# Five attention blocks of a fused transformer stack: the wait of an element's first scores is split, and its second part stands at the middle unit

## The chip, the cores and the metric

The kernel is one program for one core of a Trainium2 chip. Its time is the device time of one execution in microseconds (us). Before the change three runs gave a median of 1972.47 us (1972.38 to 1973.41). A trace was taken of one further execution, which took 1972.66 us; its span from the first to the last instruction is 1970.9 us.

## The reference

Four small transformer layers run one after the other on `x` of shape (8, 112, 256): 8 batch elements of 112 tokens. Three of them also read a context of shape (8, 375, 256). Cut to what matters:

```python
def attention(q_in, kv_in):                 # per layer with its own norm, bias, head size
    q, k, v = heads(q_in @ wq), heads(kv_in @ wk), heads(kv_in @ wv)
    s = einsum('bhqd,bhkd->bhqk', q, k) / sqrt(dh)
    return merge(softmax(s, -1) @ v) @ wo

x = x + self_attention(ln(x))               # layer 0, 16 heads of 16
x = x + cross_attention(ln(x), ln(ctx))
x = x + mixture_of_8_experts_top2(ln(x))
x = x + causal_self_attention(ln(x))        # layer 1, 16 heads of 16
x = x + mlp(ln(x))
x = x + cross_attention(ln(x), ctx)
x = x + mlp(ln(x))
x = x + cross_attention(rms(x), ctx)        # layer 2, 16 heads of 64 on 4 key heads, q and k normed
x = x + swiglu(rms(x))
x = x + self_attention(rms(x))
x = x + swiglu(rms(x))
x = x + cross_attention(rms(x), rms(ctx))   # layer 3, 16 heads of 64, rotary, plus the input mask
x = x + silu_gated_mlp(rms(x))
```

All of it is in float32.

## The kernel before

The 13 lines of the reference are 13 blocks that the kernel works through in order. In the code they are `L0_sa`, `L0_ca`, `L0_moe`, `L1_sa`, `L1_m1`, `L1_ca`, `L1_m2`, `L2_ca`, `L2_m1`, `L2_sa`, `L2_m2`, `L3_ca`, `L3_m` (`sa` self attention, `ca` cross attention). Every engine has its own program and its own in-order queue; they meet through semaphores only. Nothing schedules the work: the order on each engine is that of the Python loops.

An attention block handles the 8 batch elements in turn. Work on an element is cut into units. In `L0_ca`, `L1_ca` and `L3_ca` a unit is one head, 16 units to an element; in `L2_ca` there are 12 units and in `L2_sa` 4. Step `s` of element `b` does the following, each on its own engine: TensorE (PE) computes the scores of units `s` and `s+1` at every even `s` (`scores`, lines 882 to 926; the matmuls are on L907, L912 and L902); VectorE (DVE) takes a unit's maximum (L1762, or L1751 with the mask) and, later, the reciprocal of its row sum (L1767); ScalarE (ACT) does the exponential (L1340); GpSimd (POOL) multiplies the probabilities by the reciprocal (L2102); TensorE turns them (L935), VectorE copies them back (L1776), and TensorE multiplies them by the values (L963, L968). Each of these runs some units behind the scores. In the two steps that follow the third or so, the output projection of the element before is done (L990), and VectorE adds it to X.

Between these, the pieces of the next element `b+1` are made in the steps that the table `SCHEDULES` names: `XT` and `CT0`, `CT1` turn tokens and context, `Q`, `K0`, `K1`, `QP0`, ..., `V1` are projections, and `QT0`, `QT1`, `KT0`, `KT1` are turned queries and keys. TensorE writes a piece to PSUM (`piece`), and ScalarE copies it to SBUF (evacuates it) and then increments one of the semaphores `w_done0`, `w_done1`, `w_done2`, one for each bank that the pieces share in turn. `KT0` and `KT1` are evacuated by L1320, after the exponential of the same step.

The queries and keys of an element lie in SBUF in two halves. The first half of the units reads only the first half: in the blocks with heads of 16, `qz[..., 0:4]` and `kT[..., 0]`, in the others the queries of `QT0` and the keys of `KT0` (or `K0`). The second half of the units reads only the second. In `L0_ca` and `L1_ca` the queries are spread out with a mask by two operations on GpSimd, `spread0` and `spread1` (L623), one for each half; each increments `spread`. In `L1_ca` they stand ahead of the scaling of units 11 and 13 in GpSimd's queue, in `L0_ca` ahead of 12 and 14.

At unit 0 of an element the function `scores` waits for all of this: for both spreads (`count(st["spread"], 2, b, 2)`, L889 to L890), for the evacuation of all pieces of queries and keys (`wait_evacuated`, which for each bank waits for the last piece of those named), and, in every unit, for the banks of PSUM to be free (`exped` or `maxed`). In `L1_ca` the keys come from memory (`kv_loaded`).

Of the kernel before, what the change touches and what calls it, by code (L numbers as in the profile page):

```python
# [185 lines left out]
def parity(m):  # L186
    return (m if isinstance(m, int) else m.o) % 2

def pair(m):  # L190
    return m // 2 if isinstance(m, int) else m.i + m.o // 2
# [110 lines left out]
def build(nc, x, ctx, mask, consts, rows, b2, rbias, rows_hbm, results_hbm, keys_hbm, values_hbm, attn_w, mlp_w, out):  # L302
    with ExitStack() as es:
# [3 lines left out]
        def sem(name):  # L307
            return es.enter_context(nc.semaphore(name))
# [137 lines left out]
        spread = sem("spread")  # L446
# [109 lines left out]
        def head_of(u):  # L556

            return 8 * (u // 8) + 2 * (u % 4) + u // 4 % 2

        def place(blk, u):  # L560

            if not blk.pairs or blk.keys_first:
                return u
            if blk.dh == 64:
                return 8 * (u // 8) + 4 * (u % 2) + u % 8 // 2
            return 4 * (u // 4) + (0, 2, 1, 3)[u % 4]

        def group_of(blk, s):

            if blk.pairs:  # L570
                return 2 * (s // (2 * blk.kc)) + s % 2, s % (2 * blk.kc) // 2
            return divmod(s, blk.kc)
# [10 lines left out]
        def count(base, per, b, k=0):  # L583

            if isinstance(b, int):
                return b * per + (base + k)

            return b.i * (2 * per) + max(b.o * per + base + k, 1)
# [18 lines left out]
        def evacuated(blk, st, m, name):  # L607

            w = blk.bank_of[name]
            return w_done[w], count(st[f"w{w}"], blk.in_bank(w), m, blk.in_bank(w, name) + 1)  # L610

        def wait_evacuated(eng, blk, st, m, names):

            for w in range(len(blk.w_banks)):
                mine = [x for x in names if blk.bank_of[x] == w]
                if mine:
                    eng.wait_ge(*evacuated(blk, st, m, max(mine, key=blk.pieces.index)))
# [11 lines left out]
        def wait(eng, s, value):  # L629
            if isinstance(value, int) and value <= 0:  # L630
                return
            eng.wait_ge(s, value)
# [158 lines left out]
        def _(pe):  # L791
# [4 lines left out]
            def attention(n):  # L796
                blk, st = BLOCKS[n], START[n]
                warm = WARM.get(blk.name, {})
                spare = 7 if blk.out_bank != 7 else blk.w_banks[1]
                np_, units, gu, lag = len(blk.pieces), blk.units, blk.gu, blk.lag  # L800
# [82 lines left out]
                def scores(b, s):  # L883

                    n = 2 if blk.pairs else 1
                    free = masked if blk.mask == "causal" else maxed if blk.mask else exped
                    base = st["masked"] if blk.mask == "causal" else st["turn"] if blk.mask else st["unit"]
                    wait(pe, free, count(base, units, b, s + n - blk.s_banks))
                    if s == 0 and blk.dh == 16 and blk.cross:  # L889
                        pe.wait_ge(spread, count(st["spread"], 2, b, 2))  # L890
                    if s == 0 and blk.ahead:
                        pe.wait_ge(kv_loaded[parity(b)], pair(b) * 32 + 32)
                    if s == 0:

                        wait_evacuated(pe, blk, st, b, [x for x in blk.pieces if x in ("Q", "Q0", "Q1", "K0", "K1", "QT0", "QT1", "KT0", "KT1")])
                    if blk.pairs:
                        for z in range(2):
                            bank = blk.bank_at(s + z)
                            if blk.keys_first:
                                g, q = group_of(blk, s + z)  # L900
                                rows = slice(64 * z, 64 * z + 64)
                                mm(ps[0:blk.kp, bank, 0:HG * S], kT[rows, parity(b), g // 2, q * blk.kp:(q + 1) * blk.kp],  # L902
                                   qz[rows, parity(b), 4 * (g // 2):4 * (g // 2) + 4], start=True, stop=True).then_inc(scored, 1)
                            elif blk.dh == 16:
                                h = head_of(place(blk, s + z))
                                rows = slice(64 * z, 64 * z + 64)
                                mm(ps[0:S, bank, 0:blk.nk], qz[rows, parity(b), 4 * (h // 8) + h % 4],  # L907
                                   kT[rows, parity(b), h // 8, 0:blk.nk], start=True, stop=True).then_inc(scored, 1)
                            else:
                                u = place(blk, s + z)  # L910
                                rows = slice(64 * z, 64 * z + 64)
                                mm(ps[0:S, bank, 0:blk.nk], qz[rows, parity(b), 4 * (u // 8) + u % 4],  # L912
                                   kT[rows, parity(b), u // 8, 0:blk.nk], start=True, stop=True).then_inc(scored, 1)
                        return
                    if blk.keys_first:
                        g, q = divmod(s, blk.kc)
                        mm(ps[0:blk.kp, blk.bank_at(s), 0:HG * S], kT[:, parity(b), g // 2, q * blk.kp:(q + 1) * blk.kp],
                           qz[:, parity(b), HG * g:HG * (g + 1)], start=True, stop=True).then_inc(scored, 1)
                        return
                    for i in range(blk.heads):  # L920
                        u = s * blk.heads + i
                        last = mm(ps[0:S, blk.bank_at(s), i * blk.nk:(i + 1) * blk.nk],
                                  qz[:, parity(b), head_of(u) if blk.dh == 16 else u],
                                  kT[:, parity(b), u // 8, 0:blk.nk], start=True, stop=True)
                    last.then_inc(scored, 1)
# [82 lines left out]
                def body(b):  # L1008
                    for s in steps(b, blk, blk.out_step + 1):
                        if b == B and s in warm.get("tail", {}):  # L1010
                            keep_busy(spare, warm["tail"][s])
                        if b != B and (s % 2 == 0 or not blk.pairs):
                            scores(b, s)
                        at = lagged(b, s, lag, units)
                        if at and not blk.keys_first:
                            turn(*at)
                        if b == B and feeds(n) and s == lag - 1 + blk.keys_first:
                            pe.wait_ge(exped, START[n + 1]["unit"])
                            keep_busy(spare, warm.get("tokens", 0))
                            for b2_ in range(SOON):  # L1020
                                turn_tokens(n + 1, b2_)
                        at = lagged(b, s, lag + 1 - blk.keys_first, units)
                        if blk.keys_first and s == blk.out_step and b != 0:
                            project(b + -1, min(b + 1, B) if isinstance(b, int) else b + 1)
                        if at and at[1] % (gu * blk.wg) == gu * blk.wg - 1:
                            weigh(at[0], at[1] // gu)
                        if not blk.keys_first and s == blk.out_step and b != 0:
                            project(b + -1, min(b + 1, B) if isinstance(b, int) else b + 1)
                        if more(b):
                            for name in blk.plan.get(s, []):  # L1030
                                piece(b + 1, name, count(st["out"], 1, b) if name not in blk.early else None)
# [1278 lines left out]
```

## Time and profile before

| | us |
|---|---|
| median of three runs | 1972.47 |
| the profiled execution | 1972.66 |
| its span | 1970.9 |
| TensorE busy in the span | 1742.6 (88%) |
| VectorE busy | 1298.0 (66%) |
| ScalarE busy | 843.0 (43%) |
| GpSimd busy | 705.1 (36%) |

The five attention blocks that the change touches stand at these places (us from the start of the span; engine columns are busy time, the last is the clock granted to TensorE, 1.00 being its full 2.4 GHz):

| block | stretch | length | TensorE | VectorE | GpSimd | clock |
|---|---|---|---|---|---|---|
| `L0_ca` | 139 to 353 | 214 | 194.97 | 154.89 | 115.86 | 0.98 |
| `L1_ca` | 782 to 950 | 168 | 147.36 | 143.07 | 113.51 | 1.00 |
| `L2_ca` | 1030 to 1260 | 230 | 215.57 | 136.20 | 80.19 | 1.00 |
| `L2_sa` | 1353 to 1505 | 152 | 128.30 | 107.69 | 5.12 | 0.92 |
| `L3_ca` | 1600 to 1890 | 290 | 261.13 | 190.49 | 148.71 | 0.98 |

A wait costs time where the engine that waits sets the pace and nothing behind it has room to spare. So the rows to read are those of an element's first scores: what TensorE did before them, how long it stood idle, and what released it.

### The profile page before, as it was taken

To read this page: it belongs to the slowest core of one execution; us is meant where nothing else is said; L and a number is where in the kernel's file an instruction comes from. 1 tells how busy PE (TensorE), PEld (TensorE's weight loads), DVE (VectorE), ACT (ScalarE), POOL (GpSimd) and SP (SyncE) were. 2 spreads that over 40 slices of the span, in tenths; PEclk is the share of its full clock that TensorE was granted. 3 is DMA by queue.
4 is the path that set the end of the run, shared out by engine and by line. 5 is a ranking of instruction groups with operands and counts; after the bars stand their busy time and mean duration, and the time that the engine had idled before them with its cause. 6 is when DMAs were issued, how large, how long until landed. Compare 5 with 4: busy or idle time off the path is not lost.

```text
span 1970.9 us, 35184 instructions
## 1 busy us (share of the span) xinstructions
PE 1742.6 (88%) x11106; PEld 1235.4 (63%) x11106; DVE 1298.0 (66%) x3310; ACT 843.0 (43%) x2473; POOL 705.1 (36%) x796
## 2 busy tenths in 40 slices
PE   5979998889997888988799999898888989999998
PEld 4756665679975667555674444585445955555567
DVE  5866677511137876888775565896778966666675
ACT  3645554333335643666324443342232445445431
POOL 2325555220022234676423332340001435555443
PEclk9989999789998989999999999999999989999999
DMA  4100000388961001102100020101001000000200
GB/s 173 37 23 13 16 8 16 108 293 323 322 230 69 0 1 32 33 31 74 70 9 17 16 72 0 54 1 65 0 0 61 16 1 13 23 11 11 75 1 19
DMA packets 37006, 115.13 MB, mean 58 GB/s; under 512 B 3345, under 2 KB 23729, under 8 KB 29729
## 3 DMA queue, kind: packets, MB, share of 16 engines
q1 hardware_dynamic: 34352, 107.33, 15.7%
q0 software_dynamic: 2544, 6.43, 1.0%
q8 instruction: 59, 0.97, 0.2%
q14 instruction: 51, 0.41, 0.1%
HBM read 99.34 MB, written 14.40 MB: 58 GB/s over the span
## 4 chain that ended last, share of the span: by engine, by line
PE 41%; DVE 20%; issue 18%; POOL 14%; ACT 4%; DMA 2%; DVEq 0%; POOLq 0%; SPq 0%; ACTq 0%
POOL arena L2102 10%; PE ps L1057 6%; PE ps L1097 5%; PE ps L1207 4%; PE ps L1219 4%; PE ps L862 3%; PE ps L990 2%; PE ps L857 2%; PE ps L968 2%; DVE arena L1784 2%; PE ps L842 2%; ACT arena L1340 2%; PE ps L902 1%; PE ps L935 1%; PE ps L835 1%
## 5 line engine op out<-in xcount | busy, mean ns | idle before, releaser
L2102 POOL TENSOR_TENSOR arena<-arena,rinv 112x375 f32<-112x375 f32 (+1 forms) x448 | 370.6, 829 | 470.4 <-DVE rinv L1767 459.7
L935 PEld LDWEIGHTS ps<-cst,arena 112*125 112x125 f32 (+1 forms) x1408 | 183.8, 180 | 167.7 <-POOL arena L2102 81.9
L935 PE MATMUL ps<-cst,arena 112*125 112x112 f32 (+1 forms) x1408 | 242.6, 289 | 39.6 <-POOL arena L2102 36.5
L1340 ACT ACTIVATE arena<-ps,negmax 112x375 f32<-112x375 f32 (+1 forms) x384 | 190.3, 501 | 159.2 <-DVE negmax L1762 158.8
L1776 DVE COPY arena<-ps 125x336 f32<-125x336 f32 x384 | 190.4, 496 | 39.3 <-PE ps L935 37.8
L1762 DVE TENSOR_REDUCE negmax<-ps 112x1 f32<-112x375 f32 (+1 forms) x288 | 158.1, 549 | 69.2 <-PE ps L907 61.9
L1340 ACT ACTIVATE arena<-arena,negmax 112x112 f32<-112x112 f32 (+1 forms) x256 | 125.5, 491 | 138.9 <-DVE negmax L1751 93.0
L1057 PE MATMUL ps<-h_split_sb,w_split_sb 128*128 128x448 f32 x768 | 171.9, 371 | 7.7 <-DVE h_split_sb L1620 3.0
L1057 PEld LDWEIGHTS ps<-h_split_sb,w_split_sb 128*128 128x128 f32 x768 | 145.0, 190 | 23.8 <-POOL w_split_sb L2178 4.9
L857 PE MATMUL ps<-wat,arena 128*125 128x256 f32 (+1 forms) x576 | 145.3, 388 | 8.9 <-ACT arena L1279 7.5
L990 PE MATMUL ps<-wat,arena 128*112 128x256 f32 x512 | 126.5, 392 | 9.4 <-DVE arena L1786 3.7
L2178 POOL TENSOR_TENSOR w_split_sb<-wml,w_split_sb 128x512 fp32r<-128x512 f32 (+1 forms) x40 | 46.4, 1161 | 243.8 <-ACT w_split_sb L1406 241.9
L907 PE MATMUL ps<-arena 64*112 64x375 f32 x512 | 114.6, 525 | 16.9 <-ACT arena L1340 9.3
L1784 DVE RECIPROCAL arena<-ps 128x448 f32<-128x448 f32 x32 | 94.5, 2952 | 50.7 <-PE ps L976 50.7
L857 PEld LDWEIGHTS ps<-wat,arena 128*125 128x125 f32 (+1 forms) x576 | 101.5, 187 | 38.4 <-issue 17.0
L1097 PE MATMUL ps<-g_split_sb,w_split_sb 128*128 128x448 f32 x480 | 111.2, 368 | 5.0 <-DVE g_split_sb L1909 5.0
L990 PEld LDWEIGHTS ps<-wat,arena 128*112 128x112 f32 x512 | 87.1, 179 | 39.0 <-issue 8.4
L1767 DVE RECIPROCAL rinv<-rowsum 112x1 f32<-112x1 f32 (+1 forms) x448 | 70.2, 157 | 56.9 <-PE ps L912 48.0
L1097 PEld LDWEIGHTS ps<-g_split_sb,w_split_sb 128*128 128x128 f32 x480 | 89.3, 188 | 15.9 <-DVE g_split_sb L1909 8.9
L968 PE MATMUL ps<-arena,vz 125*64 125x448 f32 (+1 forms) x448 | 94.9, 550 | 3.7 <-DVE arena L1786 3.2
L862 PE MATMUL ps<-wat,arena 128*112 128x512 f32 x192 | 94.4, 625 | 1.7 <-DVE X L1943 1.4
L1495 ACT ACTIVATE arena<-ps,wml 128x128 f32<-128x128 f32 x168 | 47.8, 369 | 96.6 <-PE ps L1207 96.6
(230 smaller groups left out, 3262.6 us busy)
## 6 DMA issues: line engine op xcount, KB each, us to landing
wml<-in_wm_L_moe SPq DMA_DIRECT2D x21, 1028.0 KB, 7.2
wml<-in_wm_L_moe SPq DMA_DIRECT2D x21, 1024.0 KB, 8.2
craw<-in_ctx SPq DMA_DIRECT2D x32, 375.0 KB
wml<-in_wm_L_m SPq DMA_DIRECT2D x3, 3072.0 KB, 13.8
wat<-in_wa_L_ca SPq DMA_DIRECT2D x2, 2560.0 KB, 9.6
wml<-in_wm_L_m SPq DMA_DIRECT2D x2, 2048.0 KB, 9.9
keys_hbm<-arena SPq DMA_DIRECT2D x8, 375.0 KB
arena<-keys_hbm SPq DMA_DIRECT2D x8, 375.0 KB
```

The source lines that it names most:

```text
L857: last = mm(ps[0:blk.kp, W_BANK, i * D:(i + 1) * D], kv[:, k2, q * blk.kp:(q + 1) * blk.kp], w[:, k2], start=k2 == 0, stop=k2 == DC - 1)
L862: last = mm(ps[0:S, W_BANK, :], hT[:, k2], wq[:, k2, i * 512:(i + 1) * 512], start=k2 == 0, stop=k2 == DC - 1)
L935: last = nc.tensor.transpose(ps[0:blk.kp, T_BANK + s % blk.t_banks, o:o + S], buf[:, i * blk.nk + q * blk.kp:i * blk.nk + (q + 1) * blk.kp ...
L968: last = mm(ps[64 * z:64 * z + 64, O_BANK, 0:HG * S], vz64[0:kp, par, q, (g - 1 + z) * 64:(g + z) * 64], pT[0:kp, (g - 1 + z) % 4, q], sta ...
L990: last = mm(ps[0:S, blk.out_bank, blk.out_at:blk.out_at + D], oT[:, c], wo[:, c], start=c == 0, stop=c == blk.cq - 1)
L1057: last = mm(out, w[:, k2, v], h_split_sb[:, h, k2, tokens], start=k2 == 0 and i == 0, stop=k2 == DC - 1 and i == 2)
L1097: last = mm(ACC(c, half), w[:, c * P:(c + 1) * P], g_split_sb[:, t % 2, g], start=f == 0 and i == 0, stop=f == FC - 1 and i == 2)
L1340: last = go(probs[0:S, s % blk.nprobs, i * nk:(i + 1) * nk], src[:, i * nk:(i + 1) * nk], ACT.Exp, scale=-1.0 if blk.mask == "input" else ...
L1762: v.tensor_reduce(negmax[:, s * blk.heads:(s + 1) * blk.heads], src, AX_X, ALU.max, negate=True).then_inc(maxed, 1)
L1776: last = v.tensor_copy(pT[0:kp, place(blk, s) // gu % 4, :, place(blk, s) % HG], T_[:, 0:KC * S].rearrange("p (k s) -> p k s", s=S))
L1784: v.reciprocal(inverse, ps[:, L_BANK, 0:HG * S]).then_inc(inverted, 1)
L2102: pool.tensor_tensor(p3, p3, r3, ALU.mult).then_inc(scaled, 1)
```

## The change

At unit 0 the first scores wait for the first `spread` and for `Q`, `K0`, `QT0`, `KT0` only. The middle unit (`units // 2`) waits for the second `spread` and for `K1`, `QT1`, `KT1`. Nothing else is edited; later lines move down by three, so that L907 becomes L910, L912 L915 and L935 L938.

```diff
                     wait(pe, free, count(base, units, b, s + n - blk.s_banks))
-                    if s == 0 and blk.dh == 16 and blk.cross:
-                        pe.wait_ge(spread, count(st["spread"], 2, b, 2))
+                    if s in (0, units // 2) and blk.dh == 16 and blk.cross:
+                        pe.wait_ge(spread, count(st["spread"], 2, b, 1 + (s > 0)))
                     if s == 0 and blk.ahead:
                         pe.wait_ge(kv_loaded[parity(b)], pair(b) * 32 + 32)
                     if s == 0:
 
-                        wait_evacuated(pe, blk, st, b, [x for x in blk.pieces if x in ("Q", "Q0", "Q1", "K0", "K1", "QT0", "QT1", "KT0", "KT1")])
+                        wait_evacuated(pe, blk, st, b, [x for x in blk.pieces if x in ("Q", "K0", "QT0", "KT0")])
+                    elif s == units // 2:
+
+                        wait_evacuated(pe, blk, st, b, [x for x in blk.pieces if x in ("K1", "QT1", "KT1")])
```

No instruction of VectorE, ScalarE, GpSimd or SyncE changes, and no matmul changes its place. What moves are waits on TensorE. In `L3_ca`, the first scores of an element in the loop stand like this before (L912 the scores, L935 the turned probabilities, `w_done0` the bank of `KT1`, `w_done1` that of `KT0`):

```order
L935 MATMUL ps<-cst,arena 125x112 [waits turned,scaled]
L935 MATMUL ps<-cst,arena 125x112 x2
L577 UNCONDITIONAL_BRANCH
L577 ISA
L617 ISA [waits maxed]
L617 ISA [waits w_done0]
L912 MATMUL ps<-arena 112x375 [waits w_done1]
L912 MATMUL ps<-arena 112x375
```

and like this in the changed kernel:

```order
L938 MATMUL ps<-cst,arena 125x112 [waits turned,scaled]
L938 MATMUL ps<-cst,arena 125x112 x2
L577 UNCONDITIONAL_BRANCH
L577 ISA
L617 ISA [waits maxed]
L915 MATMUL ps<-arena 112x375 [waits w_done1]
L915 MATMUL ps<-arena 112x375
```

The wait on `w_done0` is gone from unit 0. It stands at unit 8, where the scores read `[waits maxed]` before and `[waits w_done0,maxed]` now.

In `L1_ca` the wait on `spread` at unit 0 stays where it is with a value that is lower by one, so that its rows read alike. The new one stands at unit 8. Before (L907 the scores, L963 the product with the values, L929 and L952 registers for the waits that follow):

```order
L935 MATMUL ps<-cst,arena 125x112 [waits turned,scaled]
L935 MATMUL ps<-cst,arena 125x112 x2
L632 REGISTER_ALU
L907 MATMUL ps<-arena 112x375 [waits exped]
L907 MATMUL ps<-arena 112x375
L929 REGISTER_ALU
```

and in the changed kernel:

```order
L938 MATMUL ps<-cst,arena 125x112 [waits turned,scaled]
L938 MATMUL ps<-cst,arena 125x112 x2
L632 REGISTER_ALU
L890 REGISTER_ALU [waits exped]
L910 MATMUL ps<-arena 112x375 [waits spread]
L910 MATMUL ps<-arena 112x375
L932 REGISTER_ALU
```

One instruction in TensorE's queue came to it, and the matmul's own wait is now that on `spread`.

## Rows read from the trace of the kernel before

**Rows 1.** Who waited for whom, TensorE in `L1_ca`: total us, times, longest us

```profile
PE ps L907 <- POOL arena L623: 6.9, 7, 1.1
```

**Rows 2.** Who waited for whom, TensorE in `L3_ca`

```profile
PE ps L912 <- ACT arena L1320: 5.2, 7, 0.8
```

**Rows 3.** Timeline, turn to element 3 of `L1_ca`: start us, us, what, [idle before <-releaser]

```profile
837.91 0.94 POOL L623 TENSOR_TENSOR arena<-qs,cst 128x448 f32<-128x448 f32 x1
...
839.62 0.91 PE L935 MATMUL ps<-cst,arena 112*125 112x112 f32 x6
...
840.34 0.94 POOL L623 TENSOR_TENSOR arena<-qs,cst 128x448 f32<-128x448 f32 x1
...
841.24 1.58 POOL L2102 TENSOR_TENSOR arena<-arena,rinv 112x375 f32<-112x375 f32 x2
...
841.51 0.89 PE L907 MATMUL ps<-arena 64*112 64x375 f32 x4 [0.98 <-POOL arena L623]
...
842.42 0.55 DVE L1762 TENSOR_REDUCE negmax<-ps 112x1 f32<-112x375 f32 x1 [0.75 <-PE ps L907]
...
843.12 0.81 POOL L2102 TENSOR_TENSOR arena<-arena,rinv 112x375 f32<-112x375 f32 x1 [0.30 <-DVE rinv L1767]
```

**Rows 4.** Timeline, later in element 2 of `L1_ca`

```profile
828.34 0.55 DVE L1762 TENSOR_REDUCE negmax<-ps 112x1 f32<-112x375 f32 x1 [0.30 <-PE ps L907]
...
829.93 0.89 PE L907 MATMUL ps<-arena 64*112 64x375 f32 x4
...
832.48 0.78 PE L963 MATMUL ps<-arena,vz 125*32 125x112 f32 x24 [1.15 <-DVE arena L1776]
```

**Rows 5.** Timeline, turn to element 3 of `L3_ca`

```profile
1708.89 0.47 ACT L1320 ACTIVATE arena<-ps 128x375 f32<-128x375 f32 x1
...
1709.86 0.08 DVE L1751 DVE_READ_ACCUMULATOR2_ANT negmax<- 112x1 f32 x1
...
1709.96 0.48 PE L935 MATMUL ps<-cst,arena 112*125 112x112 f32 x3
...
1710.58 0.46 ACT L1320 ACTIVATE arena<-ps 128x375 f32<-128x375 f32 x1
...
1711.17 0.89 PE L912 MATMUL ps<-arena 64*112 64x375 f32 x4 [0.73 <-ACT arena L1320]
...
1712.28 0.16 DVE L1767 RECIPROCAL rinv<-rowsum 112x1 f32<-112x1 f32 x1 [0.97 <-PE ps L912]
...
1717.29 0.88 DVE L1573 TENSOR_SCALAR arena<-craw,ctx_rstd_rms 125x256 f32<-125x256 f32 x3 [1.36 <-DMA craw<-in_ctx]
...
1720.31 0.16 DVE L1767 RECIPROCAL rinv<-rowsum 112x1 f32<-112x1 f32 x1 [1.20 <-PE ps L912]
```

**Rows 6.** Timeline, turn to the last element of `L3_ca`

```profile
1860.36 0.89 PE L912 MATMUL ps<-arena 64*112 64x375 f32 x4 [0.70 <-DVE negmax L1751]
```

**Rows 7.** Timeline, entry of `L3_ca`

```profile
1603.07 0.99 ACT L1320 ACTIVATE arena<-ps 128x375 f32<-128x375 f32 x2 [1.55 <-PE ps L879]
...
1606.01 0.55 DVE L1751 CUSTOM_DVE_ANT_0 arena<-ps,mask_sb 112x375 f32<-112x375 f32 x1 [0.54 <-PE ps L912]
```

**Rows 8.** Timeline, turn to element 3 of `L0_ca`, and its middle unit

```profile
214.35 0.94 POOL L623 TENSOR_TENSOR arena<-qs,cst 128x448 f32<-128x448 f32 x1
...
217.12 0.89 PE L907 MATMUL ps<-arena 64*112 64x375 f32 x4
...
228.39 0.89 PE L907 MATMUL ps<-arena 64*112 64x375 f32 x4
```

**Rows 9.** Timeline, a turn of elements in `L2_ca` and in `L2_sa`

```profile
1116.45 1.02 PE L902 MATMUL ps<-arena 64*125 64x448 f32 x4 [0.65 <-ACT arena L1320]
...
1390.79 1.01 PE L902 MATMUL ps<-arena 64*112 64x448 f32 x4
```

**Rows 10.** Line 632 in `L1_ca`, TensorE's queue: times, ns min/median/max

```profile
L632 PEldq EVENT_SEMAPHORE  x130: 51/51/51, 785.2 to 948.7; - x130
...
L632 PEldq ALU_OP  x60: 32/32/32, 799.6 to 921.8; - x60
```

## The prediction

> **What bounds the kernel now.** I read the view of waits first, for TensorE and one block at a time, because the change touches nothing but waits on TensorE. Two waits of the kind that the change removes stand in it. In `L1_ca` the scores on L907 waited 7 times for a spread on GpSimd, 6.9 us in all [rows 1]. In `L3_ca` the scores on L912 waited 7 times for L1320, which copies the turned keys out of PSUM, 5.2 us in all [rows 2]. An element has 7 successors in a block, so these are waits of once per element. Then I read the timeline around one turn of elements in each of the five blocks, to see whether the idle time is TensorE's alone or passes on to the engines that follow. The reader is to see there the bracket behind a row: idle time of that engine before it, and what released it.
>
> **`L1_ca`, the term of spreads.** At the turn to element 3 the last matmuls of element 2 end at 839.62 + 0.91 = 840.53. The first scores start at 841.51, 0.98 us later, released by the spread that ran from 840.34 to 841.28 [rows 3]. That is `spread1`, which units 8 to 15 read. `spread0`, all that unit 0 needs, ended at 837.91 + 0.94 = 838.85, well before. So the first scores start at once after the matmuls, 0.98 us earlier.
>
> Does the time get through? The next in line is VectorE: it stood idle 0.75 us before the maximum of unit 0 [rows 3], so it can start only 0.75 us earlier, being busy until then. Its work then runs without a gap until, some 7 us on, it waits for TensorE again, by 0.30 us [rows 4]. The other 0.23 us are within those 0.30, so from there on VectorE too is 0.98 early, provided TensorE kept its lead meanwhile. TensorE does not stand idle for VectorE in this part; its next such wait is the one of 1.15 us at 832.48, after the output of the element before [rows 4], and what it waits for there is work that TensorE itself set going. I allow 0.03 to 0.05 us a turn for waits on VectorE's copies that are now just in time, and take 0.95. GpSimd is no bound either, since it waited 0.30 us for a reciprocal right behind the turn [rows 3], and VectorE's lead reaches it later in the element. If it were the bound, 0.30 a turn would be all that is gained, which is the lower end. The upper end is the whole wait, 6.9 us. Seven turns: 7 x 0.95 = 6.6 us, between 7 x 0.30 = 2.1 and 6.9.
>
> **`L3_ca`, the term of turned keys.** The matmuls before the turn end at 1709.96 + 0.48 = 1710.44; the first scores start at 1711.17, after `KT1` was copied (1710.58 + 0.46 = 1711.04) [rows 5]. `KT0`, all that unit 0 needs, was copied at 1708.89 + 0.47 = 1709.36. The other wait of unit 0 is for the maximum of unit 14, which frees its bank; that was done at 1709.86 + 0.08 = 1709.94. Both lie before 1710.44, so 0.73 us go whole. VectorE stood idle 0.97 us behind it [rows 5], more than the 0.73, and follows in full. Six turns are of this kind. The seventh, to the last element, has 0.70 us [rows 6]; the row names the maximum, which like ScalarE's copy belongs to the waits of that one matmul, and I read it as the same case. The first entry in rows 2 is the block's entry, not a turn. Sum 6 x 0.73 + 0.70 = 5.1 us.
>
> One thing in this block does not move with TensorE: the context of the next element. Its load is started by the last maximum of the element before, which the change leaves where it is, and VectorE waited 1.36 us for it at 1717.29 [rows 5]. It will wait 0.73 longer. Behind that stall, though, VectorE had 1.20 us to spare until the scores of unit 4 at 1720.31 [rows 5]. 1.20 - 0.73 = 0.47 us are left, so the stall stays hidden. I take 5.1, with nothing as the lower end if that cover fails.
>
> At the entry of the block the two copies of keys take 0.99 us from 1603.07, so half of it, 0.5 us, is no longer waited for; VectorE had 0.54 us idle behind it [rows 7]. 0.5 us, between 0 and 0.54.
>
> **The other three blocks.** In `L0_ca` the second spread ended at 214.35 + 0.94 = 215.29 and the first scores started at 217.12 with no idle time before them: TensorE was still on the last projections of the values [rows 8]. `K1` is copied before the exponential of unit 14, for which unit 0 waits anyway. Gain 0. In `L2_ca` there is a wait for L1320, 0.65 us at the turn shown [rows 9], and it looks like that of `L3_ca`, but the table makes `KT1` at step 9 and `KT0` at step 10: the half that unit 0 needs comes last, and ScalarE works in order. The wait stays whole. In `L2_sa` the copy of `QT1` is no longer waited for, but TensorE multiplies the values after that piece and came to the scores at 1390.79 with no idle time [rows 9]. Gain 0.
>
> **The added waits.** Each element now has two more waits in `L0_ca` and `L2_ca` and one more in `L1_ca`; in `L2_sa` and `L3_ca` one moves. That is 8 x (2 + 2 + 1) = 40 more. In TensorE's queue a wait with its register took 51 + 32 = 83 ns [rows 10], so 40 x 0.083 = 3.3 us if nothing covers them. They are covered: at the middle unit TensorE came to the scores with its array still busy, 228.39 in `L0_ca` [rows 8] and 829.93 in `L1_ca` [rows 4], and what is waited for was ready some 10 us before. I take 0, and 3.3 as the upper end.
>
> The Trainium skill (Advanced Engine Details and Errata, Miscellaneous Facts, Network/Comms) puts the reading of a semaphore by a sequencer on this chip at 50 to 100 ns, which speaks against adding 40 of them. The trace agrees with its lower end, with the 51 ns of rows 10. By the page's upper end, as an estimate, the 40 would come to 4 us if nothing hid them.
>
> **The sum.** 6.6 + 5.1 + 0.5 = 12.2 us. The profiled execution took 1972.66 us, 0.19 more than the median of the runs, so 1972.66 - 12.2 = 1960.5 us.
>
> **Rivals.**
> 1. *GpSimd paces `L1_ca`.* For it: it does 113.51 us of work in 168 us there and is the line on which most of the chain of waits in this block runs. Then a turn gives 0.30 instead of 0.95, 2.1 us in the block: 1972.66 - 2.1 - 5.1 - 0.5 = 1965.0. Against it: most of its rows there have idle time before them, ended by a reciprocal.
> 2. *The context load paces `L3_ca`.* Cover of 0.47 us is little, and the load's landing varies by some tenths. Then the block's turns give nothing: 1972.66 - 6.6 - 0.5 = 1965.6.
> 3. *Both, or the turns give their time back further on* in some resource that the turn does not show: 1972.66 - 2.1 - 0.5 = 1970.1, which can't be told from no change. That the change misses its aim altogether would look the same; against that stand the two sums in the view of waits.
> 4. *Slower, by the waits at the middle unit.* [...] At the turn in rows 3 the first scores came 0.23 us after the spread's end (841.51 - 841.28), with three such waits in the queue. If each of the 40 new waits cost that much, it would be 40 x 0.23 = 9.2 us, and with rival 3's gain of 2.6 the time would be 1972.66 - 2.6 + 9.2 = 1979.3. It decides if TensorE stands idle before the middle scores for more than 0.17 us per new wait (40 x 0.17 = 6.8, the gain of 2.6 plus 0.2% of the time). Against it: no idle time before the middle scores in rows 4 and 8.
>
> **How the numbers follow.** A measurement of this kernel can tell 0.2%, 3.9 us, from no change. Forecast 0.64, rival 1 0.10, rival 2 0.11, rival 3 0.11, rival 4 0.04. Faster: forecast and rivals 1 and 2, 0.85; same: rival 3, 0.11; slower: rival 4, 0.04. The forecast's own range is 1957.5 to 1963.8: all waits gone whole (6.9 + 5.1 + 0.54 = 12.5, and a little for where the runs lie) at one end, 12.2 less 3.3 for the waits at the other. The range asked for takes in rivals 1 and 2 and leaves out 3 and 4, 0.15: 1957.5 to 1967.
>
> **What would show it.** In the changed trace the scores of L910 at the turns of `L1_ca` have no idle time before them that a spread ends, and turns follow each other in 20.05 us instead of 21.0 (841.51 less 0.98 is the first of them). In `L3_ca` L915 does not wait for L1320, and VectorE's wait for the context at step 2 is about 2.1 us. `L2_ca` still shows its waits for L1320. No bracket stands before the scores of a middle unit. The prediction is wrong if `L1_ca` is shorter by less than 5 us, which would mean that VectorE or GpSimd took over; if `L3_ca` is, by less than 4, the load is the first to look at; and if a bracket does stand before the middle scores, the waits are not free.

## The result, and the profile after

The changed kernel takes 1957.55 us (median of 4 runs, 1957.03 to 1957.92) where the kernel before, beside it, takes 1972.43. The ratio is 0.9922, 95% interval 0.9909 to 0.9934: 14.9 us less, where 12.2 were forecast. Two later comparisons on other chips gave 0.993 (0.9915 to 0.9945 and 0.9916 to 0.9945), some 13.8 us. The forecast of 1960.5 us is a ratio of 0.9939: inside the two later intervals, just outside the first. The measured 1957.55 us lies at the very edge of the forecast range, 1957.5 to 1967.

The page of the changed kernel: its span, and the costliest group of scores.

```profile
span 1956.0 us, 35237 instructions
PE 1741.5 (89%) x11106; PEld 1234.9 (63%) x11106; DVE 1296.8 (66%) x3310; ACT 842.1 (43%) x2473; POOL 704.9 (36%) x796
L910 PE MATMUL ps<-arena 64*112 64x375 f32 x512 | 116.7, 534 | 9.9 <-ACT arena L1343 8.6
```

Each engine's work is the same within 1.2 us; what went is idle time, 9.9 us before L910 where the page of before has 16.9 for the same group. Line numbers behind the edit are higher by three than before the change (L902 is now L905).

The view of waits, TensorE in `L1_ca` and then in `L3_ca`: total us, times, longest us.

```profile
PE ps L966 <- DVE arena L1779: 7.6, 7, 1.1
PE ps L910 <- ACT arena L1343: 0.7, 1, 0.7
PE ps L938 <- DVE arena L1779: 0.6, 3, 0.2
PE ps L910 <- issue: 0.4, 2, 0.2
...
PE ps L915 <- DVE negmax L1754: 0.3, 1, 0.3
```

The 6.9 us of [rows 1] and the 5.2 of [rows 2] are gone. What is new is small: 0.6 us for copies that are now just in time, and 0.4 before the first scores of two elements.

The timeline of the changed kernel, turn to element 3 of `L1_ca`, against [rows 3].

```profile
836.03 0.91 PE L938 MATMUL ps<-cst,arena 112*125 112x112 f32 x6
...
836.75 0.94 POOL L623 TENSOR_TENSOR arena<-qs,cst 128x448 f32<-128x448 f32 x1
...
837.10 0.89 PE L910 MATMUL ps<-arena 64*112 64x375 f32 x4 [0.17 <-issue]
...
839.06 1.08 DVE L1577 TENSOR_SCALAR xn<-X,mv,rstd 112x256 f32 x1
...
841.23 0.55 PE L938 MATMUL ps<-cst,arena 112*125 112x112 f32 x3 [0.18 <-DVE arena L1779]
```

The scores start at 837.10, while `spread1` still runs (836.75 + 0.94 = 837.69). The change is in this row: half of the queries are not there yet, and unit 0 doesn't wait for them. The turns of the block start at 796.98, 816.92, 837.10, 857.44, 877.67, 897.96 and 917.90, which is 20.15 us apart on the average; before they were 20.98 apart (799.48 to 925.38).

The same for `L3_ca`, against [rows 5]: the turn to element 3, VectorE's wait for the context, and the next scores.

```profile
1698.46 0.89 PE L915 MATMUL ps<-arena 64*112 64x375 f32 x4
...
1700.01 0.48 PE L938 MATMUL ps<-cst,arena 112*125 112x112 f32 x3
...
1700.42 0.89 PE L915 MATMUL ps<-arena 64*112 64x375 f32 x4
...
1700.63 0.46 ACT L1323 ACTIVATE arena<-ps 128x375 f32<-128x375 f32 x1
...
1701.53 0.16 DVE L1770 RECIPROCAL rinv<-rowsum 112x1 f32<-112x1 f32 x1 [0.18 <-PE ps L915]
...
1707.31 0.88 DVE L1576 TENSOR_SCALAR arena<-craw,ctx_rstd_rms 125x256 f32<-125x256 f32 x3 [2.12 <-DMA craw<-in_ctx]
...
1709.57 0.16 DVE L1770 RECIPROCAL rinv<-rowsum 112x1 f32<-112x1 f32 x1 [0.43 <-PE ps L915]
```

The copy of `KT1` (1700.63) now runs beside the first scores. The wait for the context has grown from 1.36 to 2.12 us and the cover behind it has shrunk from 1.20 to 0.43. Five turns, from 1628.11 to 1808.96, are 36.17 us apart, where they were 36.96 apart (1637.27 to 1822.09).

### The profile page after: what moved, and what is told of

Its sections match the earlier page's. It is cut to its first block, busy times and chain, and to the rows that moved or that the text cites. A ratio compares the mean times of both kernels' runs of the same rounds, so it can differ in the third digit from the quotient of the medians.

```text
span 1956.0 us, 35237 instructions
## 1 busy us (share of the span) xinstructions
PE 1741.5 (89%) x11106; PEld 1234.9 (63%) x11106; DVE 1296.8 (66%) x3310; ACT 842.1 (43%) x2473; POOL 704.9 (36%) x796
## 4 chain that ended last, share of the span: by engine, by line
PE 47%; DVE 20%; issue 15%; POOL 10%; ACT 4%; DMA 2%; DVEq 0%; POOLq 0%; SPq 0%; ACTq 0%
POOL arena L2105 7%; PE ps L1060 6%; PE ps L1100 5%; PE ps L1210 4%; PE ps L938 4%; PE ps L1222 4%; PE ps L862 3%; PE ps L910 3%; PE ps L993 2%; PE ps L857 2%; PE ps L971 2%; PE ps L966 2%; DVE arena L1787 2%; PE ps L835 2%; PE ps L842 2%
## 5 line engine op out<-in xcount | busy, mean ns | idle before, releaser
L938 PEld LDWEIGHTS ps<-cst,arena 112*125 112x125 f32 (+1 forms) x1408 | 185.8, 182 | 167.4 <-POOL arena L2105 89.1
L938 PE MATMUL ps<-cst,arena 112*125 112x112 f32 (+1 forms) x1408 | 244.7, 291 | 38.0 <-POOL arena L2105 36.9
L910 PE MATMUL ps<-arena 64*112 64x375 f32 x512 | 116.7, 534 | 9.9 <-ACT arena L1343 8.6
L966 PE MATMUL ps<-arena,vz 125*32 125x112 f32 (+1 forms) x2048 | 78.4, 273 | 12.7 <-DVE arena L1779 11.5
## 6 DMA issues: line engine op xcount, KB each, us to landing
wml<-in_wm_L_m SPq DMA_DIRECT2D x3, 3072.0 KB, 13.8
```

What stands on the lines that cost most here:

```text
L938: last = nc.tensor.transpose(ps[0:blk.kp, T_BANK + s % blk.t_banks, o:o + S], buf[:, i * blk.nk + q * blk.kp:i * blk.nk + (q + 1) * blk.kp ...
```

## The experiments

Each kernel was timed against the kernel before on the same chip, 4 to 12 executions each, and one execution was traced. The ratios are these:

| kernel | ratio | 95% interval |
|---|---|---|
| only_L1_ca | 0.996 | 0.9947 to 0.9973 |
| only_L3_ca | 0.9952 | 0.994 to 0.9965 |
| all_but_two | 0.9998 | 0.9989 to 1.0006 |
| after_again, after_third | 0.993, 0.993 | 0.9915 to 0.9945, 0.9916 to 0.9945 |
| two_blocks | 0.994 | 0.9924 to 0.9957 |
| added_waits | 0.9998 | 0.9988 to 1.0007 |
| spreads_earlier | 0.998 | 0.9968 to 0.9991 |
| filler_tail | 0.9927 | 0.9908 to 0.9946 |
| kt0_first, kt0_first_again | 0.9902, 0.990 | 0.9887 to 0.9917, 0.9883 to 0.9918 |
| kt0_and_filler | 0.99 | 0.9884 to 0.9916 |

The traces tell more than these intervals of some 5 us. For each I took four lengths, from an element's first scores to another's: `L1_ca` (its first scores to those of `L2_ca`), `L2_ca` (to those of `L2_sa`), `L2_sa` (to those of `L3_ca`), and `L3_ca` (its first scores to its last). So what is won at the entry of `L2_ca` stands in the column of `L1_ca`, and what is won at the entry of `L3_ca` in that of `L2_sa`. The table has each length less that of before (251.73, 320.11, 250.33 and 278.84 us). In brackets is the low clock met there: I read the granted clock in stretches of 2 us, counted each where its middle lies, and summed what was missing to 1.00 over those under 0.97, in us. A dip below is a stretch in which the granted clock was at its lower level, 1.2 GHz or 0.5 of the full one.

| trace | `L1_ca` | `L2_ca` | `L2_sa` | `L3_ca` |
|---|---|---|---|---|
| before | 0 (3.4) | 0 | 0 (12.5) | 0 (6.4) |
| added_waits | -0.48 (3.6) | -0.02 | -0.81 (11.3) | -0.37 (5.7) |
| all_but_two | +0.05 (3.4) | -0.38 | +0.06 (12.6) | +2.40 (7.8) |
| spreads_earlier | -3.90 (6.8) | +0.11 | -1.58 (10.6) | +0.08 (6.5) |
| only_L1_ca | -5.99 (5.1) | +0.05 | -1.25 (12.3) | -2.87 (3.0) |
| only_L3_ca | -0.11 (3.4) | -0.09 | +0.08 (12.8) | -5.99 (4.3) |
| two_blocks | -5.89 (4.0) | +2.41 | -2.29 (10.7) | -8.00 (2.9) |
| the changed kernel | -5.18 (8.5) | +0.21 | -2.26 (10.8) | -6.25 (4.5) |
| after_again | -5.34 (5.1) | -0.23 | -2.15 (10.1) | -7.58 (3.4) |
| after_third | -5.52 (3.4) | -0.35 | -0.53 (12.5) | -7.40 (2.8) |
| filler_tail | -5.86 (4.0) | +2.49 | -1.92 (10.8) | -6.56 (4.6) |
| kt0_first | -6.45 (3.4) | -4.46 | -2.21 (10.2) | -7.67 (3.4) |
| kt0_first_again | -6.63 (3.4) | -3.54 | +0.90 (14.3) | -6.05 (4.3) |
| kt0_and_filler | -6.39 (3.4) | -4.29 | -2.08 (10.3) | -7.62 (3.4) |

In `L2_ca` only three traces met a dip, at its entry or in the block: two_blocks and filler_tail, each with 3.4 us missing, are the two that are 2.4 and 2.5 us longer there; kt0_first_again has 1.7 us missing. The stretch ahead of `L1_ca` is in no column. The first scores of `L1_ca` came between 1.4 us earlier (the changed kernel) and 3.7 us later (kt0_first) than before, and added_waits, without the split, came 1.3 earlier. Of the edits only the one in `L0_ca` acts there, and from the first scores of that block's first element to those of its last it is 184.6 or 184.7 us in all fourteen traces.

**The parts.** Four kernels, the first three with the split in some blocks only. They differ in the name list of one condition:

```diff
+                    split = blk.name in ("L1_ca",)     # ("L3_ca",) / ("L0_ca", "L2_ca", "L2_sa")
-                    if s in (0, units // 2) and blk.dh == 16 and blk.cross:
-                        pe.wait_ge(spread, count(st["spread"], 2, b, 1 + (s > 0)))
+                    if (s == 0 or split and s == units // 2) and blk.dh == 16 and blk.cross:
+                        pe.wait_ge(spread, count(st["spread"], 2, b, 1 + (s > 0) if split else 2))
```

and likewise for `wait_evacuated`.

> The split only in L1_ca; the other four blocks as before. The whole change gained 14.9 us where 12.2 were forecast. Theory A (the terms add up, and the rest is the clock or blocks I priced at nothing): the seven turns of L1_ca give 7.4 us up to its last turn, as they did in the changed kernel (925.38 to 917.90, of which 1.4 were there when the block began, so 6.1 its own), and the kernel gains 4.5 to 6.5 us: 1966.0 to 1968.0. Theory B (the surplus is L1_ca's, by something that it sets going further on): it gains 8 us or more. If the lower clock in the tail of L1_ca (scores of 1.3 to 1.6 us instead of 0.89 in the changed kernel) comes from the higher load in this block, it is seen here too, with the tail 2 us longer than before.

Measured: 0.996, about 7.9 us less, between theory A's 4.5 to 6.5 and theory B's 8 or more, and the interval of 5.3 to 10.5 takes in both. In the trace `L1_ca` gained 5.99 us, theory A's 6.1; 1.25 us more came in `L2_sa` and 2.87 in `L3_ca`, blocks that this kernel leaves as they were. The trace's total, 9.2 us, is theory B's, but not its cause: the 2.87 go with 3.0 us of low clock instead of 6.4 in `L3_ca`, and a gain in `L2_sa` does not follow the split in `L1_ca` (kt0_first_again, with it, is 0.90 longer there). The tail met a dip more than the kernel before (5.1 us missing instead of 3.4), but from the last element's first scores on it took 108.56 us and before 108.49, so the tail is not the 2 us longer that the text expected.

> The split only in L3_ca. Theory A: turns of 36.17 us instead of 36.97, 7 x 0.80 less 0.1 at the last, and 0.5 at the entry: 6.1 us, so 1966.3. Theory B (the size in my forecast, from the idle time in brackets, was right and the rest came from elsewhere): 5.1 + 0.5 = 5.6 us, turns of 36.24. In both the stages before L3_ca are as before the change, within 0.3 us.

Measured: 0.9952, about 9.5 us less (6.9 to 11.8): more than either theory's 6.1 or 5.6. The trace can't say where the excess is, since the execution that was traced was only 4.8 us faster than that of before. In it the turns are 36.17 us apart (1637.72 to 1818.55), theory A's figure; `L3_ca` is 5.99 us shorter, and the three lengths before it are as before within 0.1 us.

> The split in L0_ca, L2_ca and L2_sa, where I priced it at nothing, and not in L1_ca and L3_ca. Theory A1 (these blocks gain, unforeseen: 1.4 us between the end of L0_ca and the experts, 1.6 us in the first element of L2_sa): 2 to 3 us less than before, 1969.5 to 1970.5, with the first layer of the experts 1.4 us early. Theory A2 (those two differences belong to the granted clock, which differed between the two traces there, and not to the change): within 1 us of before. Rival 4 of the prediction (the added waits cost something): slower than before by 1 us or more.

Measured: 0.9998. Theory A2 stands: these three blocks gain nothing that can be measured, and the experts' first layer, which the changed kernel reached 1.7 us early, is 1.5 us late here, and 3.2 us early in added_waits, which has no split at all. The waits cost nothing that can be measured either, so rival 4 falls.

> The changed kernel once more, for a second trace of it. If the differences in the stages without a planned gain (1.4 us at the entry of the experts, 2 us lost in the tail of L1_ca, 1.6 us at the start of L2_sa) belong to the change, they stand here again within 0.3 us; if they are the clock's from one execution to the next, at least one is gone or has another size, and the sum still comes to 14.5 to 15.3 us below before.

Measured: 0.993. At the experts the lead is 0.7 us, and in the third trace 0.4, instead of 1.7: that one is of the execution. The 2 us in `L2_sa` came again, and were 0.53 in the third trace.

**The split in the two blocks alone, and two repeats beside it.** The same edit with the names `L1_ca` and `L3_ca`.

> The split in L1_ca and L3_ca alone, without it in L0_ca, L2_ca and L2_sa. Theory (the gain is these two blocks' turns, and what else differs is how many dips of the granted clock an execution meets): the ratio to before is that of the whole change, 0.9922 to 0.993, and L2_sa, with its old wait, is 2 us shorter than before as in the changed kernel, since it meets one dip less there. Rival: L2_sa's own split brings those 2 us; then L2_sa is as long as before the change and the ratio is about 0.994.

Measured: 0.994. The ratio is the rival's figure, and its interval takes in both; this trace also met the dips in `L2_ca` that cost it 2.4 us. `L2_sa` decides: with its old wait it is 2.29 us shorter. Here are both kernels from the start of `L2_sa` to that of `L3_ca`, first before, then this one. The columns are the stretch, its length, the busy time of TensorE, its weight loads, VectorE, ScalarE and GpSimd with their instructions, the granted clock, and the DMA's share and rate.

```profile
1354.00:1602.00 248.00, 214.62 (x988) 142.50 (x988) 190.91 (x370) 84.57 (x177) 31.56 (x30) 0.95 0.04 16
```

```profile
1353.60:1600.00 246.40, 212.97 (x988) 141.39 (x988) 191.06 (x370) 84.69 (x177) 31.66 (x30) 0.96 0.04 16
```

The same 988 matmuls took TensorE 214.62 us and 212.97, at a clock of 0.95 and 0.96; VectorE's work is the same. The rival, that the split in `L2_sa` brings the 2 us, falls. What does bring them is one dip less in `L2_sa` and the entry of `L3_ca` (shown below), whose first scores end this length.

> The changed kernel for a third time, beside kt0_first_again on the same chip. Expected at 0.992 to 0.993 of before. Turns of L3_ca 36.2 us apart, those of L1_ca 19.9 to 20.4.

Measured: 0.993; as expected.

**The added waits alone.** Unit 0 waits for everything as before, and the middle unit waits too:

```diff
-                    if s == 0 and blk.dh == 16 and blk.cross:
+                    if s in (0, units // 2) and blk.dh == 16 and blk.cross:
                         pe.wait_ge(spread, count(st["spread"], 2, b, 2))
...
+                    elif s == units // 2:
+                        wait_evacuated(pe, blk, st, b, [x for x in blk.pieces if x in ("K1", "QT1", "KT1")])
```

> The kernel before with the 40 added waits of the middle units alone; unit 0 waits for everything as before. Theory: they cost nothing, since TensorE's queue reaches them while its array is still busy: within 1 us of before, and no idle time before the scores of the middle units. Rival 4 of the prediction: up to 3.3 us slower if nothing hides 83 ns each, 9.2 us slower if each costs 0.23 us.

Measured: 0.9998, and in its trace 6.8 us of waiting for the spreads at the turns of `L1_ca` as before, with no new bracket. In this kernel the 40 waits cost nothing that can be measured (-0.12% to +0.07%).

**The same wait removed in another way.** The kernel before, with one line of its table changed:

```diff
-        pool={11: ["spread0"], 13: ["spread1"]},
+        pool={10: ["spread0"], 12: ["spread1"]},
```

> The kernel before with its old wait for both spreads, but in L1_ca the spreads stand one unit earlier in GpSimd's queue (units 10 and 12 instead of 11 and 13). It takes most of the same wait away without touching the waits on TensorE. Theory: spread1 ends one scaling (0.79 us) earlier, the 0.98 us fall to about 0.2 and a turn is 0.8 us or a little more shorter: 5.5 to 6 us less than before, 1966.5 to 1967.5 by before's 1972.4. Rival 1 of the prediction (GpSimd paces the block): no more than 2 us, since its work stays the same.

Measured: 0.998, about 3.9 us (1.8 to 6.3), less than expected. The wait for a spread is gone from TensorE, with no edit of its waits. Two rows of the view of waits in `L1_ca`, of this kernel:

```profile
PEld ps L935 <- POOL arena L2102: 17.2, 33, 0.5
DVE negmax L1762 <- PE ps L907: 7.5, 15, 3.7
```

and of the kernel before:

```profile
PEld ps L935 <- POOL arena L2102: 13.6, 25, 0.5
DVE negmax L1762 <- PE ps L907: 11.0, 21, 2.2
```

VectorE waits 3.5 us less for the first scores and TensorE's weight loads 3.6 us more for the scaled probabilities, since the spreads now stand ahead of a scaling that is wanted sooner. Turns are 20.41 us apart (801.97 to 924.42): 0.57 won of 0.83. Rival 1, that GpSimd's work bounds the block to 2 us, falls by the turns (7 x 0.57 = 4.0); that its order has a price does not.

**Fillers in the tail of `L1_ca`.** In the changed kernel:

```diff
                             if at and at[1] % (gu * blk.wg) == gu * blk.wg - 1:
+                                if blk.name == "L1_ca" and b == B - 1 and s > 2:
+                                    keep_busy(spare, 5)
                                 weigh(at[0], at[1] // gu)
```

> The changed kernel, with 5 matmuls on the identity (some 0.14 us each at the high clock) ahead of the four products with the values in the last element of L1_ca, where TensorE stands idle for VectorE's copies (0.9 to 1.3 us). In three traces with the split in L1_ca the clock was granted at the low level between 932 and 950, in three without it not. Theory: the idle time there brings the clock down, and the split moved it into a less lucky place; with the fillers the scores on L910 in 930 to 945 take 0.89 us throughout, and L1_ca ends 1 to 2 us earlier than in the changed kernel. Rival: the fillers come in the way of the scores and the block is no shorter, or the clock falls all the same.

Measured: 0.9927, the same as the changed kernel. The stretch from 932 to 944, first in filler_tail, then in after_again, then in after_third:

```profile
932.00:944.00 12.00, 9.27 (x102) 6.34 (x106) 11.55 (x31) 5.43 (x18) 6.61 (x9) 1.00 0.01 2
```

```profile
932.00:944.00 12.00, 9.51 (x84) 5.89 (x84) 11.76 (x32) 5.44 (x17) 6.62 (x9) 0.86 0.01 2
```

```profile
932.00:944.00 12.00, 8.39 (x96) 5.25 (x92) 11.51 (x33) 5.31 (x16) 6.62 (x9) 1.00 0.01 2
```

The clock stays up in this stretch, but it does so in after_third too, which is the changed kernel without fillers; so that the fillers keep it up is not shown. The block is 0.3 to 0.7 us shorter than in the three traces of the changed kernel. VectorE is busy for 11.55 of these 12 us: it sets this stretch, not TensorE. No use is shown.

**`KT0` ahead of `KT1` in `L2_ca`.** The prediction found that its wait could not go, since the half that unit 0 needs is made last. So, in the changed kernel:

```diff
-              8: ["QT0"], 9: ["QT1", "KT1"], 10: ["KT0"]},
+              8: ["QT0"], 9: ["QT1", "KT0"], 10: ["KT1"]},
```

> The changed kernel, and in L2_ca KT0 made and copied before KT1 (QT1, KT0 in step 9, KT1 in step 10), so that the wait of the first scores for the last copy (4.5 us over 7 turns in the changed kernel, 0.65 at the turn shown) can go. Theory: start to start it is worth 0.75 a turn, 7 x 0.75 = 5.2 us less than the changed kernel, 0.27% (by the brackets it would be 4.5), and no wait of L905 for L1323. Rival: GpSimd's sums or ScalarE pace this block, then at most 1 us.

> Both edits of the two kernels above on the changed kernel. Theory: the gains add, 6 to 7 us less than the changed kernel, about 0.989 of the kernel before where the changed one was at 0.993. Rival: it is as kt0_first, within 1 us, if the fillers bring nothing.

> The changed kernel with KT0 ahead of KT1 in L2_ca, again. Theory: 7 turns of L2_ca shorter by 0.72 us, as its first trace had them (29.03 instead of 29.75 us apart): about 4.5 us less than the changed kernel beside it, 0.2 to 0.25%. Rival: no difference from the changed kernel in the timed runs, if something behind L2_ca gives the time back.

Measured: 0.9902, 0.99 and 0.990. The first stands for kt0_first, the second for kt0_and_filler, the third for the repeat. Beside the changed kernel on the same chip the repeat took 1953.92 us against 1958.84, 4.9 less, though the two intervals still touch at 0.9917. `L2_ca` is 4.5, 4.3 and 3.5 us shorter than before in the three traces, the last with a dip in it. The turn to element 2 in kt0_first:

```profile
1082.62 0.54 PE L879 MATMUL ps<-cst,arena 125*128 125x125 f32 x3
...
1083.09 1.02 PE L905 MATMUL ps<-arena 64*125 64x448 f32 x4
1083.19 0.48 ACT L1323 ACTIVATE arena<-ps 128x375 f32<-128x375 f32 x1
```

and in the kernel before:

```profile
1085.50 0.54 PE L879 MATMUL ps<-cst,arena 125*128 125x125 f32 x3
1086.69 0.65 PE L902 MATMUL ps<-arena 64*125 64x448 f32 x2 [0.65 <-ACT arena L1320]
```

From the turned keys to the scores it was 1.19 us and is 0.47: 0.72 gone, where the bracket says 0.65, and turns are 29.03 us apart instead of 29.75. Six turns of this kind are 4.3 us; the first, from element 0 to 1, gives 0.2. At the block's entry the scores come 1.20 us after the turned keys (1029.96 to 1031.16) instead of 1.75 (1032.12 to 1033.87), 0.55 more, which the table has under `L1_ca`. Together that is 5.1 us, the theory's 5.2. With the fillers added there is no further gain. By its medians kt0_first is the fastest kernel here.

## Where the prediction was right, and which step failed

**The waits go, whole.** Right in both blocks, in place and in what takes over. `L1_ca`: forecast 6.6. From the lead at the block's start (1.41 us) to that at its last turn (7.48) it gained 6.07; in the nine traces with the split the way to the last turn is 137.1 or 137.2 us, in the four with the old wait and the old order of the spreads 143.1 to 143.3. For the whole block, tail included, I fitted the length on the split and the low clock over nine traces (without spreads_earlier and filler_tail, and without the three kt0 kernels, whose column has the 0.55 us of `L2_ca`'s entry in it). It gives 5.6 us for the split, standard error 0.23. The forecast allowed 0.03 to 0.05 us a turn for copies just in time. The runs show more: the scores of elements 3 and 5, right behind the loop's branch, start 0.17 and 0.21 us late, and within element 3 the copies behind the norm at 839.06 hold TensorE 0.18 us more. The turns are 19.94 to 20.34 us, 20.15 on the average, and not 20.05. So this term was 0.6 us too large up to the last turn, and 1.0 over the block.

`L3_ca`: forecast 5.1. The same fit over all fourteen traces gives 4.7 for the split, standard error 0.31. It is made of two errors that nearly cancel. A turn is worth 0.80 and not the 0.73 of its bracket: the matmuls on L935 began at 1709.96 and the scores 1.21 us later [rows 5]; now it is 0.41 (1700.01 to 1700.42). The bracket counts from the modelled end of a group, but the next group, if nothing holds it, starts 0.07 us ahead of that end. Against this stands what rival 2 is about, the load of the context, which took back part of the gain once in seven turns. In the last element with a context to load, the changed kernel has

```profile
1816.83 0.88 DVE L1576 TENSOR_SCALAR arena<-craw,ctx_rstd_rms 125x256 f32<-125x256 f32 x3 [3.14 <-DMA craw<-in_ctx]
...
1821.89 3.62 PE L993 MATMUL ps<-wat,arena 128*112 128x256 f32 x16
...
1825.44 0.89 PE L915 MATMUL ps<-arena 64*112 64x375 f32 x4
```

The wait is 3.14 us where it is 2.12 in element 3, 1.02 more against a cover of 0.43, and the way from the scores at 1817.07 to those at 1825.44 is 8.37 us, where it is 7.98 in four of the five traces without the split (8.73 in all_but_two). It is 8.28 to 8.85 in all nine with it, so 0.3 to 0.9 us are given back. In the other elements (element 3 is shown above) the cover held, as forecast. What differs in this element is a second load: its context is asked for at 1809.54, and the 3 MB of weights of the next block 0.87 us behind it.

```profile
1809.54 0.27 SPq L672 DMA_DIRECT2D craw<-in_ctx  x1
...
1810.41 0.43 SPq L651 DMA_DIRECT2D wml<-in_wm_L_m  x1
```

From 1811 to 1817 the DMA engines moved 285 GB/s, their share 1.00; in the same place of element 3, from 1701 to 1707, it was 93 GB/s and 0.31. With the old wait the load is late there too, 2.27 us of waiting in only_L1_ca against 0.84 to 1.35 in its other elements, but the cover took it. That the weights are the cause was not tried; the two loads stand in every kernel here.

**The entry of `L3_ca`.** VectorE's 0.54 us of idle time [rows 7] is gone. The turned keys and the first maximum before, and then in the changed kernel:

```profile
1602.52 1.02 PE L879 MATMUL ps<-cst,arena 125*128 125x125 f32 x6 [1.58 <-DVE arena L1735]
...
1604.31 1.60 PE L912 MATMUL ps<-arena 64*112 64x375 f32 x4 [0.77 <-ACT arena L1320]
...
1606.01 0.55 DVE L1751 CUSTOM_DVE_ANT_0 arena<-ps,mask_sb 112x375 f32<-112x375 f32 x1 [0.54 <-PE ps L912]
```

```profile
1594.49 1.15 PE L879 MATMUL ps<-cst,arena 125*128 125x125 f32 x6 [1.58 <-DVE arena L1738]
...
1595.67 1.59 PE L915 MATMUL ps<-arena 64*112 64x375 f32 x4
...
1597.47 0.55 DVE L1754 CUSTOM_DVE_ANT_0 arena<-ps,mask_sb 112x375 f32<-112x375 f32 x1
```

From the turned keys to the first maximum it was 3.49 us and is 2.98: 0.51 gone, the forecast's 0.5. The scores themselves came 0.61 sooner (1.79 us after the keys, now 1.18); VectorE's small operations of the norm fill the time up to 1597.47. The lengths of the table are too rough to show this by themselves.

**The terms of nothing.** `L0_ca`, `L2_ca` and `L2_sa`: right within what can be measured (all_but_two). The fit gives 0.1 us for the split in `L2_sa`, standard error 0.22. The added waits: right (added_waits). In `L2_ca` L905 still waited 4.5 us for L1323, and kt0_first shows that the reason given, the order of the two halves, was the right one.

**Where the sum failed.** The step that failed is the sum itself, "1972.66 - 12.2 = 1960.5": it took it that all that no term names stays equal, and so put what the granted clock does at nothing, without a reason. The range did no better: its terms reach down to 1972.66 - 12.5 = 1960.2, and the rest of the way to 1957.5, 2.7 us, is "a little for where the runs lie". What the runs showed in its place is this. The terms, 5.6 + 4.7 and 0.5 at the entry, are 10.8 us, 1.4 less than forecast. The two traces are 14.9 us apart. In `L2_sa` and `L3_ca` together the trace of before met 18.9 us of low clock, that of the changed kernel 15.3, and by the fits each us costs 0.8 (standard error 0.09) in `L2_sa` and 1.0 (0.10) in `L3_ca`: about 3.3 us. In `L1_ca` it costs 0.1 (0.07), since VectorE sets the pace of the tail; there the changed kernel met 5.1 us more and lost some 0.5. It reached `L1_ca` 1.4 us ahead, of which the repeats show 0.2 and 0.6. 10.8 + 3.3 - 0.5 + 1.4 = 15.0.

That the forecast came so near is in part luck: its terms were 1.4 us too large together, and what it left out was more than that.

What a dip does can be seen in element 6 of `L3_ca` before the change:

```profile
1824.87 1.59 PE L912 MATMUL ps<-arena 64*112 64x375 f32 x4
...
1827.16 2.46 PE L862 MATMUL ps<-wat,arena 128*112 128x512 f32 x4
...
1831.58 0.89 PE L912 MATMUL ps<-arena 64*112 64x375 f32 x4
```

and in only_L1_ca, with the same code there:

```profile
1817.12 0.89 PE L916 MATMUL ps<-arena 64*112 64x375 f32 x4
...
1818.52 1.97 PE L862 MATMUL ps<-wat,arena 128*112 128x512 f32 x4
...
1822.45 0.89 PE L916 MATMUL ps<-arena 64*112 64x375 f32 x4
```

The clock is at its lower level from 1824.9 to 1828.3 in the one and nowhere in the other. From scores to scores it is 6.71 us in the one and 5.33 in the other.

**What stays open.** How much of the clock's part is the split's. The dips in `L2_sa` are not: six of them stand in added_waits and spreads_earlier, without any split, as in the changed kernel, seven in before as in after_third. In `L3_ca` all fourteen traces have low clock at the block's start, 3.4 or 5.1 us missing, with the split and without. But behind the first element four of the five traces with the old wait have one more dip or a double one, 2.4 to 2.9 us behind the first scores of element 6 (before, added_waits, spreads_earlier) or of element 5 (all_but_two). Only only_L1_ca has none. Of the nine traces with the split not one has it. So it is likely that the split takes this dip away, and with it the 1.4 us of the rows above, which then belong to the change by way of the clock. How it would do so was not tried.

The timed runs say the same: the three comparisons of the changed kernel, 16 executions of it, gave 14.9, 13.8 and 13.8 us, all above the 10.8 of the terms, though that lies at the edge of the two later intervals (10.8 to 16.8), and only_L3_ca gave 9.5 (6.9 to 11.8) where its terms are 5.2.

**The rivals.** 1 did not happen, though GpSimd's order cost spreads_earlier 0.26 us a turn; of 2 a part happened, in one turn of seven; 3 and 4 did not happen.

## What to carry to other kernels

Where a consumer waits at its first step for all of its input and reads half of it, compare the end of that half with the consumer's earliest start, and then ask which half is made last: the split alone did nothing in `L2_ca` until the order of its halves was turned round. Price such a wait by the distance from start to start, with a neighbour that doesn't wait as the measure, not by the idle time before it. Keep the terms of a sum apart from what the clock does beside them: a difference of a few us is read block by block, over several traces.

## What the runs showed that was not expected

- The granted clock's dips came at about the same places in fourteen traces but not in the same number: `L2_sa` met 10.1 to 14.3 us of low clock, and its length followed with 0.8 us for each. That made 3.1 us between two executions of one kernel in this block (kt0_first and its repeat).
- The low level costs in full where TensorE sets the pace and hardly at all where VectorE does. In the tail of `L1_ca` of the changed kernel the clock was at the low level for 17 us (932.7 to 949.7). The first row is of that tail, the second of the kernel before at the same distance, 14.1 us, behind its own last turn:

```profile
932.00:950.00 18.00, 17.73 (x106) 12.73 (x107) 15.71 (x40) 5.31 (x16) 11.63 (x16) 0.53 0.00 1
```

```profile
939.48:957.48 18.00, 14.21 (x127) 10.78 (x129) 16.58 (x40) 5.31 (x16) 12.66 (x17) 0.91 0.00 1
```

TensorE was busy for 17.73 us with 106 matmuls where it had done 127 in 14.21, and yet the tail, from the last turn to the first scores of `L2_ca`, is only 0.9 us longer: 109.38 instead of 108.49.

- Forty more waits in TensorE's queue, each of 51 ns by [rows 10] and most with 32 ns of register work, changed the time by less than can be measured, -0.12% to +0.07%.
